# Order of a few steps in an attention kernel: an exponential ahead of a rounding, and K's third block ahead of Q's

## The reference

```
q = heads(x @ Wq);  k = heads(ctx @ Wk);  v = heads(ctx @ Wv)
p = softmax(q k^T / sqrt(16))
x = merge(p v) @ Wo + b + x
```

## Time and profile before

| what | value |
|---|---|
| median of 3 runs | 946.02 us |
| the profiled execution, its own time | 937.91 us |
| its span, first to last instruction | 936.1 us |
| TensorE, matmuls | 901.5 us busy, 96% |
| vector engine | 686.5 us, 73% |
| scalar engine | 540.1 us, 58% |
| GpSimd | 399.6 us, 43% |
| mean granted TensorE clock | 0.998 |

### The profile page before, as it was taken

How to read it: one execution, slowest core, us unless ns; L and a number is a source line. 1 busy time by engine, 2 the same in 40 slices (tenths; PEclk the granted TensorE clock), 3 DMA queues, 4 the chain that set the end, 5 groups by cost and what they waited for, 6 DMA issues and landing times.

```text
span 936.1 us, 30582 instructions
## 1 busy us (share of the span) xinstructions
PE 901.5 (96%) x12766; PEld 692.7 (74%) x12766; DVE 686.5 (73%) x1223; ACT 540.1 (58%) x547; POOL 399.6 (43%) x227
## 2 busy tenths in 40 slices
PE   8899999999999999999899999999999999999897
PEld 5777877777787877777677787877878777777665
DVE  4875786866778776786867778686786868778566
ACT  4456565655556566566466556556565656656552
POOL 3424354533446254275543456354344625433323
PEclk9999999999999999999999999999999999999999
DMA  6213534545345544545455435444534544443442
GB/s 214 88 34 83 142 82 131 139 122 138 92 110 133 162 127 111 137 111 153 124 146 131 108 101 141 134 129 113 143 97 114 141 128 134 102 129 80 120 109 78
DMA packets 80537, 112.58 MB, mean 120 GB/s; under 512 B 21201, under 2 KB 37879, under 8 KB 80401
## 3 DMA queue, kind: packets, MB, share of 16 engines
q1 hardware_dynamic: 80400, 110.62, 44.1%
HBM read 60.24 MB, written 22.24 MB: 88 GB/s over the span
## 4 chain that ended last, share of the span: by engine, by line
PE 42%; DMA 20%; SPq 17%; DVE 10%; issue 6%; ACT 3%; POOL 1%; DVEq 0%; ACTq 0%; POOLq 0%
PE pR L305 16%; PE pR L430 8%; DMA X<-in_xT 7%; SPq L1387 6%; PE pA L377 5%; DMA X<-y 5%; PE pR L364 5%; DMA y<-X 4%; SPq L1394 3%; DMA out<-X 3%; SPq L1357 3%; ACT P L740 2%; PE pA L383 2%; DVE Oraw L1006 2%; SPq L1421 2%
## 5 line engine op out<-in xcount | busy, mean ns | idle before, releaser
L740 ACT ACTIVATE P<-pA 77x2048 f32<-77x2048 f32 x160 | 300.1, 1876 | 171.8 <-PE pA L383 171.5
L991 DVE TENSOR_REDUCE Mx<-pR 128x4 f32<-128x308 f32 (+1 forms) x480 | 258.8, 575 | 32.8 <-PE pR L364 29.8
L1250 POOL TENSOR_TENSOR On<-On,OS 128x1024 f32<-128x1024 f32 (+1 forms) x58 | 105.5, 1840 | 272.0 <-DMA OS<-rd 272.0
L305 PE MATMUL pR<-OS,Wo 128*128 128x512 f32 x638 | 168.9, 404 | 2.2 <-DVE OS L1047 1.4
L305 PE MATMUL pR<-XS,Wq 128*128 128x512 f32 x638 | 167.5, 402 | 2.6 <-POOL Wq L1236 1.5
L430 PE MATMUL pR<-P,VA 77*17 77x256 f32 x2480 | 157.0, 384 | 0.7 <-ACT P L740 0.3
L364 PE MATMUL pR<-KH,QH 32*128 32x154 f32 x1280 | 136.5, 292 | 19.1 <-ACT P L740 7.8
L364 PEld LDWEIGHTS pR<-KH,QH 32*128 32x128 f32 x1280 | 95.7, 184 | 78.1 <-issue 44.4
L377 PE MATMUL pA<-QH,KH 32*77 32x256 f32 x1280 | 145.1, 291 | 0.1
L305 PEld LDWEIGHTS pR<-XS,Wq 128*128 128x128 f32 x638 | 115.9, 189 | 29.4 <-POOL Wq L1236 1.9
L305 PEld LDWEIGHTS pR<-OS,Wo 128*128 128x128 f32 x638 | 114.1, 188 | 30.7 <-issue 3.8
(11 more groups left out here) (152 smaller groups left out, 1199.0 us busy)
## 6 DMA issues: line engine op xcount, KB each, us to landing
On<-Oraw SPq DMA_DIRECT2D x248, 64.0 KB, 2.6
OS<-rd SPq DMA_DIRECT2D x58, 256.0 KB
C<-in_cT SPq DMA_DIRECT2D x16, 616.0 KB, 7.9
X<-in_xT SPq DMA_DIRECT2D x16, 512.0 KB
y<-X SPq DMA_DIRECT2D x16, 512.0 KB, 4.1
X<-y SPq DMA_DIRECT2D x16, 512.0 KB
out<-X SPq DMA_DIRECT2D x15, 512.0 KB, 4.1
X<-in_xT SPq DMA_DIRECT2D x16, 256.0 KB
```

What stands on the lines that cost most here:

```text
L305: f = pe.matmul(p[:, :], W[:, k, c0:c0 + 128], S[:, s, :], start=(i == 0), stop=(i == len(pairs) - 1))
L740: act.activation(P[0:L, i % PR, :, :], pA[0:L, :, :], ACT.Exp, scale=float(D) ** -0.5).then_inc(p_done, 1)
L991: dve.tensor_reduce(Mx[:, :].rearrange("p (j i) -> p j i", j=4)[:, j:j + banks, i:i + 4], pR[:, bank:bank + banks, 0:2 * LK].rearrange("p ...
L1250: pool.tensor_tensor(On[rows, blocks, :], On[rows, blocks, :], recips(u, part).bitcast(F32), ALU.mult).then_inc(o_mul, 1)
```

## The change

In even units other than the first and the last, the scalar engine takes the exponential S(u, 1) before it rounds x of unit u+2. In all even units but the last, K's third block goes ahead of Q's third on TensorE, and with it the half copy on the scalar engine and the sums on the vector engine.

```
@@ tensor, even units @@
                     run(u, 2, n, 2, 0)
                     if u:
                         out(z, 2, 2)
+                    K(w, 2, 0)
                     Q(u + 2, 2, 3)
-                    K(w, 2, 0)
                     PV(u, 0, 1)
                     run(u, 3, n, 2, 0)
@@ scalar, even units @@
                         K(w, 1)
                         Q(u + 1, 1)
+                        S(u, 1)
                         split_x(u + 2)
-                        S(u, 1)
                         if u < NU - 4:
                             v_half_copy(w)
...
                     S(u, 2)
+                    k_half_copy(w)
                     q_half_copy(u + 2)
-                    k_half_copy(w)
                     o_copy(u, 0)
@@ vector, even units @@
                     maxima(n, 2, 0, 1, 2)
                     out(z, 2)
+                    k_sum(w)
                     q_sum(u + 2)
-                    k_sum(w)
                     maxima(n, 3, 0)
```

## The result

The changed kernel takes 953.98 us (median of 4 runs, 953.89 to 955.04) beside 944.94 us for the kernel before (median of 4, 942.4 to 947.88): a ratio of 1.0115, 95% interval 1.0072 to 1.0158. It is slower by about 1%. The forecast was 953 with a range of 944 to 961.

A forecast was written before the change was run, and what follows sets the result against it. TensorE was busy 96%, so only its standstills counted; even units carried one removable wait, set by the load of x. Gain 8.9, losses 15.4 and one meeting gave +7.7 us on 946.02: taken as 953 us, range 944 to 961.

The forecast's parts named there:

- The stall of `run(u,3)`: With K first, `run(u,3)` waits for the sums of Q's bank 3: 0.79 us in fifteen units, 11.9 us lost.
- Rival (c): The stall before `run(u,3)` does not appear, as vector sums and PV overlap better than reckoned: 941 us; chance 0.07.
- The gain of 8.9 us: Exponential ahead of rounding x: `run(u,2)` starts earlier, 7.1 us summed over u = 2 to 26 and 1.9 in u = 28.
- Unit 28, Q's wait of 1.35 us: In u = 28, shorter by 1.2 us before this place, Q's third block waits for XS: 1.35 us lost.
- Unit 14: Second-layer Wq remainders, behind x's on GpSimd, end 1.9 us later and Q waits; some 0.4 us more lost than elsewhere.
- Q no longer waits in the other units: With K first, Q starts at 17.2 us into the unit, 0.1 us after XS is complete: no wait, nothing to spare.
- Unit 0, K's wait for the bank: No output block covers K's wait for bank 0 in u = 0; K waits some 0.7 us, counted as loss.
- Longer from `run(u,2)` to `run(u,3)` in nine units, 1.1 us: V's half copy runs behind the rounding; 0.12 us more between the two starts in nine units that waited: 1.1 us lost.
- One meeting of L915 with the normalise, 1.2 us: Remainder of K's third block on the vector engine overlaps GpSimd's normalise and slows; one meeting taken, 1.2 us lost.
- Rival (b): K's remainder meets the normalise in most units, six to fourteen meetings at 0.8 to 2.1 us: 958 to 981; chance 0.13.
- the 8 us between the profiled run and the median: Profiled execution of the kernel before was 8.1 us faster than the timed median, 946.02; carried over unexplained into the forecast.
- Rival (a): The load of x lands later in timed runs than in the profile, hurting only the kernel before: 944 to 950; chance 0.30.

The follow-up runs named there:

- e2_k_only: Kernel before with only K's third block put ahead of Q's third; the rounding of x still precedes the exponential: 954.56 us, ratio 1.0120 to the kernel before.
- e3_banks: Changed kernel with banks exchanged, K's third block taking bank 3 and Q's third bank 0: 938.79 us, ratio 0.9957 to the kernel before.
- e1_exp_only: Kernel before with only the exponential put ahead of the rounding of x; Q's third block still precedes K's: 956.26 us, ratio 1.0134 to the kernel before.
- e8_after_late: Changed kernel with SP issuing the load of x later, behind values(u + 1), in even units: 954.57 us, ratio 1.0134 to the kernel before.
- e6_recip: Changed kernel with the addition of out(z, 0) ahead of the two reciprocals on the vector engine in even units: 950.45 us, ratio 1.0103 to the kernel before.
- e7_before_late: Kernel before with SP issuing the load of x later, behind values(u + 1), in even units: 970.28 us, ratio 1.0284 to the kernel before.

## Where the prediction was right and where not

The time (953 forecast, 953.98 measured) and its main terms hold. That it came out within a microsecond is luck: some terms were wrong in ways that happened to cancel. By the steps of the prediction:

**The stall of `run(u,3)`: right.** Forecast 0.79 us in fifteen units. Measured 0.65 or 0.66 us of idle time in fifteen waits, and with 0.07 us of lost overlap between matmuls 0.72, so 10.8 us in all where 11.9 were put. The step from sum to stage was 0.14 us (170.34 to 170.48), as in the earlier trace rows (888.21 to 888.36). `e2_k_only` shows it without the first edit, `e3_banks` takes it away by the bank alone. Rival (c) falls.

**The gain of 8.9 us: some 5.5 of it came,** counted as the prediction counts, by the starts of `run(u,2)`. The waits for the exponential are gone, as forecast. But "each unit then starts `run(u,2)` at 13.16" was the step that failed. In six units the addition L1058 releases the stage later. In five of them (4, 10, 14, 20, 24) it stands behind a reciprocal that waits 0.65 to 1.03 us for its DMA, and TensorE waits 0.19 to 0.60; at `run(u,3)` most of that was made up. In the 28th it is another thing, and the wait is the longest, 0.94 us:

```profile
840.69 0.34 PE L364 MATMUL pR<-KH,QH 32*128 32x154 f32 x2 [0.94 <-DVE X L1058]
844.86 1.41 PE L305 MATMUL pR<-XS,Wq 128*128 128x512 f32 x5 [0.25 <-POOL XS L1218]
```

The waits of before had no row for this, since a wait for two things is put down to the later one. The timeline has the row that would have told for unit 28 (vector engine, before):

```profile
829.86 0.75 DVE L1058 SCALAR_TENSOR_TENSOR X<-pR,bias,X 128x512 f32<-128x512 f32 x1
```

That is 12.13 to 12.88 into the unit, as in most units, right behind the output block (z, 0), which ends at 829.82 and has filled bank 3. In the other units V's block lies over this addition; in unit 28 there is none, so `run(28,2)` could not start at 12.0 but at 13.0, and 0.8 of the 1.9 us could be had. Unit 6 had a late addition too (done at 13.44), hidden under the wait for the exponential. In the five units above, the trace of before had L1058 done at 12.86 to 13.02, in time: that the DMA of the row sums would land later there was not to be read from it, only that it can. I did not ask when every other thing that `run(u,2)` needs is done.

With the price of the second edit removed, the gain can be read alone. The prediction's own terms then leave 6.0 us (8.9 less 1.35, 0.4 and 1.1). `e3_banks` is 4.1 us below the kernel before by their ratio (0.0043 of 943.38). The sum of TensorE's waits fell from 26.7 to 23.7 us, and eight overlaps of 0.08 are 0.6 more: 3.6 us. In it 7.8 us for the exponential went, against 3.3 that came for L1058; the other rows moved both ways (L991 ahead of L364 from 2.2 to none, L1047 from 1.4 to 3.9, and smaller ones).

**Unit 28, Q's wait of 1.35 us: wrong, and the same step.** Since `run(28,2)` itself came 0.94 us late, Q waited only 0.25 us (second line of the first fence above). The two errors belong together. **Unit 14:** Q's wait for the remainders of Wq was 1.9 us against 1.5 before, the 0.4 that was forecast.

**Q no longer waits in the other units: right**, and by as little as forecast. XS is ready at 17.15 and Q starts at 17.3 to 17.5 (in unit 18, which is late as a whole, at 18.80 and 18.95). `e1_exp_only` shows the 0.87 us per unit that K in Q's place hides.

**Unit 0, K's wait for the bank: 0.7 forecast,** 1.03 us of waiting measured instead of the 0.32 of the earlier trace rows, which is 0.7 more. **Longer from `run(u,2)` to `run(u,3)` in nine units, 1.1 us:** in unit 4 the distance grew from 6.14 to 6.76 us, 0.62, less than the stall alone, because the late start of `run(4,2)` was made up. In units 2, 8, 12 and 26, where `run(u,2)` starts on time after the change, it grew from some 6.15 to some 7.09, by 0.90 to 0.96. With 0.72 for the stall, 0.2 is left for this term, and the rows show the half copy of V behind it (L975 done at 14.40, the second pair of `run(u,2)` at 14.46). The term was real; no experiment separates it.

**One meeting of L915 with the normalise, 1.2 us: two came,** with 0.96 and 1.59 us of waiting. In unit 12, which starts at 374.05, the normalise was early: 22.1 into the unit, where the others have 22.6 to 23.9 (unit 18, late as a whole, 26.3), and L915 at 21.9 to 22.2 as in most. In unit 14 (start 431.4) Q and all behind it were late by the wait for Wq, and L915 came at 24.4, after the normalise at 23.9; it had met it before, too. In `e3_banks`, where `run(u,3)` and with it L915 run some 0.7 us earlier, none is left but the one of the start, in unit 0. The normalise itself stayed where it was against the output block on the whole: it starts 6.21 us behind its end in unit 4 and 6.24 in unit 22 (6.05 and 5.69 before, from the trace of before), with a median of 6.5 (before 6.4). Unit by unit it did not stay: in unit 12 it came 5.8 behind instead of 7.8, and that made the meeting there; unit 22, the only one that the prediction had under 5.98, had none. The other traces with L915 at this place say the same: `e8_after_late` has two, in units 8 and 22, and `e2_k_only` and `e6_recip` none. So the term is a draw from run to run, of none to two meetings. Rival (b) falls with two of fourteen; `e1_exp_only`, with `run(u,3)` 0.4 us later, has three, fewer than the five more that the prediction had put on 0.3 us.

**Not in the sum at all:** waits for L1006 in front of score stages of odd units, 2.8 us against 1.1, and for L1047 3.3 against 1.4. In `e3_banks` the first is 1.6 and the second 3.9, though that kernel is faster; so I can't say that L1047's waits are the change's.

The balance of the two traces closes. All rows of TensorE's waits add up to 26.7 us before and 38.7 after, 12.0 more: L961 +9.8, L1058 +2.8, L1047 +1.9, L1006 +1.7, L1062 +1.0, L991 in front of L364 +0.6 and in front of K and Q +0.7, exponential in front of L364 -7.8, and 1.3 in smaller ones. Of the 16.1 us between the spans of the two profiled runs (936.1 and 952.2), some 3.6 are the clock by the line above (0.998 and 0.994); half a microsecond is left for lost overlap.

**The forecast itself.** I carried the 8 us between the profiled run and the median over as it was, without a reason. That gave the right time, and it was a guess: the sum (+7.7) was made of terms within one clock, and the timed medians differ by 9.0. Rival (a), which would have put that offset into the landing, had a chance of 0.30. That was too much, since the granted clock of 0.998 stood in the profile and pointed elsewhere, though one run couldn't say how far.

## What to carry to other kernels

Before an order is changed to get a tight operand out of the way, look at which bank the moved step fills and who takes that bank next. Here the order change alone lost 1%, and the same order with two bank numbers exchanged gained 0.4%. When a wait is taken away, its gain ends at the next thing that the same instruction needs, and the trace shows that only by the end of each other producer, not in the list of waits. Lay the sum against runs of the same granted clock, since one profiled run may differ from the median by its clock alone.

## What the runs showed of the hardware

**Time goes with the granted clock from run to run.** Between 0.988 and 1.0 of mean granted clock the same kernel took 951 to 937 us, 0.89 us per 0.001. A clock that merely scaled all of TensorE's 900 us would give 0.9, so the size fits. What lowers the clock is shown in part: in `e7_before_late`, with 17.9 us more of waiting for the exponential, its low stretches come with the longest of these waits, and the six runs had 0.978 to 0.990. But `e3_banks`, with no such wait, had 0.991 to 0.997, much like the kernel before, so these waits aren't all of it.

**The vector engine and GpSimd on SBUF.** L915 with both operands in SBUF takes 0.37 us alone; under the normalise one of them took up to 2.51 (2.80 us for two in unit 12, 3.46 in unit 14). What a long one has in common, here and in the casts below, is its end: 0.14 to 0.19 us behind the end of the GpSimd operation that it met (in unit 12 L915 runs from 396.28 to 398.79, the first normalise from 396.14 to 398.62). L915 at 395.99, which was there first, kept its 0.37. In `e3_banks` another small operation met it at times, the cast of Q from its half sums. Operations of the cast's line in that kernel (shortest, median and longest in ns):

```profile
L944 DVE CAST QH<-Qt x32: 277/295/2212, 26.5 to 891.5; 128x256 fp32r<-128x256 f32 x32
L944 DVE CAST QH<-pR x15: 675/691/692, 64.6 to 841.6; 128x512 fp32r<-128x512 f32 x15
```

The cast from SBUF is 0.30 us in the median and 2.21 at most; the one from PSUM, twice the size, never left 0.68 to 0.69, though only one of the fifteen, at 176.0, lay wholly under a GpSimd operation. In unit 22 a cast from SBUF took 1.41 us (at 674.03, with the normalise from 671.66 to 675.29). `e3_banks` has eleven such casts of 0.5 us and more, and no row of TensorE waiting for the maxima (L991) in front of a score stage; the meetings of L915 in the changed kernel cost it 0.96 and 1.59 us.
